# A second pick for the seven hottest tiles in a graph network kernel

## The reference, cut to what matters

```python
# first: attention of a kind, over the edges (row = src, col = dst)
h1   = relu(h[row] @ W1[:d] + h[col] @ W1[d:] + b1)
mask = sigmoid(h1 @ W2 + b2)[:, 0]
w    = mask / (segment_sum(mask, row)[row] + 1e-09)
agg  = segment_sum(w[:, None] * h[col], row)
out  = relu(where(deg > 0, 0.5 * h + 0.5 * agg, h) @ Wl + bl)
# second: four graph convolutions with a maximum over the neighbours
for W, R in (first, second, second, second):
    agg = segment_max(h[src], dst);  agg = where(isneginf(agg), 0, agg)
    h   = relu(agg @ W + b + h @ R)
```

## Time and profile before

| | before |
|---|---|
| median of three runs | 5941.76 us (5936.39 to 5943.95) |
| the profiled execution's own time | 5939.93 us |
| its span in the trace | 5938.1 us |
| busy: PE, DVE, POOL, ACT | 3743.0, 4317.3, 3295.4, 869.0 us |
| granted TensorE clock, mean | 0.869 |
| indirect gathers into `c_ring` | 1720 |
| gathers into `c_far_rows` | 16, 4 a layer |

### The profile page before, as it was taken

The page is one execution under the profiler, slowest core; times in us unless marked ns, Lnnn a source line. Parts: engine busy times, 40 slices in busy tenths (PEclk is TensorE's granted clock), DMA queues, the critical chain, the costliest instruction groups (busy, mean ns, idle before and its releaser), DMA issues. The chain is left out here.

```text
span 5938.1 us, 52093 instructions
## 1 busy us (share of the span) xinstructions
PE 3743.0 (63%) x16577; PEld 1793.4 (30%) x16577; DVE 4317.3 (73%) x7131; ACT 869.0 (15%) x2470; POOL 3295.4 (55%) x3349
## 2 busy tenths in 40 slices
PE   6670010565555542899997777757875777757775
PEld 5430010222222211444443333323332333323332
DVE  7789981876666652888886776758876887767775
ACT  0010001100000002777764100010000100010000
POOL 0210002477777774333332777767776777767776
PEclk9999995787878776999998888879998999978887
DMA  0129943644434434999997533334333433343332
GB/s 17 31 102 420 421 177 85 175 147 118 122 118 123 125 96 80 194 196 190 192 184 142 139 118 111 114 96 135 118 118 101 131 118 116 123 103 118 112 112 71
DMA packets 355334, 817.99 MB, mean 138 GB/s; under 512 B 95420, under 2 KB 209810, under 8 KB 354755
## 3 DMA queue, kind: packets, MB, share of 16 engines
q0 software_dynamic: 146496, 329.42, 25.5%
q1 hardware_dynamic: 159172, 406.54, 19.4%
q10 hardware_dynamic: 49392, 78.70, 4.6%
HBM read 579.98 MB, written 234.41 MB: 137 GB/s over the span
## 5 line engine op out<-in xcount | busy, mean ns | idle before, releaser
L2087 PE MATMUL c_wide<-c_choice,c_parts 128*128 128x512 fp8e4 (+1 forms) x8232 | 1766.9, 372 | 667.5 <-DVE c_even L2175 277.0
L1962 POOL DMA_INDIRECT c_ring<-table,near x1720 | 1649.3, 959 | 524.1 <-issue 523.5
L2087 PEld LDWEIGHTS c_wide<-c_choice,c_parts 128*128 128x128 bf16 x8232 | 810.6, 102 | 1598.9 <-issue 337.9
L2175 DVE TENSOR_TENSOR c_even<-c_even,c_wide 128x896 f32<-128x896 f32 x672 | 727.6, 1083 | 62.9 <-PE c_wide L2087 57.5
L2175 DVE TENSOR_TENSOR c_odd<-c_odd,c_wide 128x896 f32<-128x896 f32 x644 | 697.5, 1083 | 82.0 <-PE c_wide L2087 77.2
L2190 DVE TENSOR_REDUCE c_staged<-c_ring 128x128 f32<-128x1024 f32 (+15 forms) x196 | 400.4, 2043 | 413.2 <-DMA c_ring<-table,near 412.9
L1312 PE MATMUL a_wide<-a_choice,a_parts 128*128 128x512 fp8e4 (+1 forms) x2058 | 486.7, 385 | 337.6 <-DVE a_hidden L1398 312.6
L1702 PE MATMUL b_agg<-b_mass,b_h_row 128*128 128x512 f32 (+1 forms) x1372 | 592.9, 572 | 164.6 <-DMA b_mass<-masks 164.2
L1663 ACT ACTIVATE b_mass<-b_onehot,mask_r 128x128 f32<-128x128 bf16 x2058 | 625.5, 388 | 259.2 <-DVE b_onehot L1725 259.0
L1646 POOL DMA_DIRECT2D b_mass<-masks x343 | 296.4, 866 | 607.5 <-ACT b_mass L1663 580.2
L1191 POOL DMA_INDIRECT a_ring<-table_a,near x430 | 458.7, 1067 | 286.6 <-issue 130.4
(11 more groups left out here) (281 smaller groups left out, 3558.4 us busy)
## 6 DMA issues: line engine op xcount, KB each, us to landing
masks<-n_zeros SPq DMA_DIRECT2D x196, 784.0 KB, 15.2
b_mass<-masks POOLq DMA_DIRECT2D x343, 448.0 KB, 7.5
c_choice<-chosen SPq DMA_DIRECT2D x196, 784.0 KB
a_pick_row<-picks ACTq DMA_DIRECT2D x343, 224.0 KB, 3.7
chosen<-a_choice SPq DMA_DIRECT2D x49, 784.0 KB, 5.2
c_ring<-table,near POOLq DMA_INDIRECT x1720
c_source<-table SPq DMA_DIRECT2D x28, 448.0 KB, 6.5
a_ring<-table_a,near POOLq DMA_INDIRECT x430, 2.9
```

The source lines that it names most:

```text
L1962: pool.indirect_dma_start(ring[:, at + j, :], None, table1[layer % 2], bass.IndirectOffsetOnAxis(near[:, u, j:j + 1], 0)).then_inc(landed[ ...
L2087: last = pe.matmul(wide[q][:, lo_c:hi_c], parts[:, s, part, :], choice[e][:, s % CHUNK, lo_c:hi_c], start=(part == 0), stop=(part == 2))
L2175: dve.tensor_tensor(side[:, :], side[:, :], found, ALU.max).then_inc(taken, 1)
```

## The change

Four things change together.

- **A second pick.** The seven hottest tiles, one in each range, pick a second neighbour in each tile of sources. Their 7 x 128 columns form an eighth range, so `SELECTS` becomes 392. Their caps fall from 25, 16, 15, 14, 13, 13, 12 to 10, 8, 7, 7, 6, 6, 6, and `CAP_ALL` from 430 to 372. `list_again` removes the second picks from `near`, and `pick_again` finds them for `picks`. In stage B each range gets seven more blocks, which need no part of `masks`. In stage C the eighth range is done first in each layer (`range_at`), kept in `best_hot`, and put in by the second `take` of each other range.
- **Own rows by rank.** Stage B scatters `x` and `h1` by rank to `own_x` and `own_h` (`store_rows`, 98 indirect DMAs on POOL), in place of SP's store of `own1`. In layers 0 and 3 of stage C SP loads them with plain DMAs (`load_own`), in place of POOL's 98 gathers.
- **Lists that begin early.** `block_fetched` is split into seven semaphores, and DVE waits for the one that its pair of tiles needs.
- The ring of stage A shrinks from 38 entries to 36.

```diff
-CAP_BY_RANK = ((25, 16, 15, 14) + (13,) * 2 + (12,) * 3 + (11,) * 4 + (10,) * 5 + (9,) * 6 + (8,) * 6 + (7,) * 5
+CAP_BY_RANK = ((10, 8, 7, 7) + (6,) * 3 + (12,) * 2 + (11,) * 4 + (10,) * 5 + (9,) * 6 + (8,) * 6 + (7,) * 5
                + (6,) * 5 + (5,) * 4 + (4,) * 3 + (3, 2))
+ALL_RANGES = RANGES + 1
+ALL_TILES = TILES + RANGES
...
-                dve.wait_ge(block_fetched, TILES * 16)
                 for pair in range(0, TILES, 2):
                     both = range(pair, min(pair + 2, TILES))
+                    dve.wait_ge(block_fetched[both[-1] // PASS], PASS * 16)
...
+                hot = near[:, :, :].rearrange("p (a c) j -> p a c j", c=RANGE)[:, :, 0, :]
+                def list_again():
...
+                    for r in range(NEAR_ROUNDS):
+                        for a in range(RANGES):
+                            own.did(dve.max(top[:, a, 8 * r:8 * r + 8], work[r % 2][:, a, :]))
+                        if r < NEAR_ROUNDS - 1:
+                            for a in range(RANGES):
+                                own.did(dve.match_replace(work[1 - r % 2][:, a, :], top[:, a, 8 * r:8 * r + 8],
+                                                          work[r % 2][:, a, :], 0.0))
...
+                def pick_again():
+                    full = [P, PASS, RANGES * NEAR]
+                    for i in range(PASSES):
+                        tiles = slice(i * PASS, (i + 1) * PASS)
+                        own.did(dve.tensor_tensor(here[0][:, :, :], bc(hi_up[:, :].unsqueeze(1), full),
+                                                  bc(up_row[:, tiles].unsqueeze(2), full), ALU.is_equal))
+                        own.did(dve.tensor_tensor(here[1][:, :, :], here[0][:, :, :],
+                                                  bc(lo_up[:, :].unsqueeze(1), full), ALU.mult))
...
+                list_again()
...
+                own.did(dve.scalar_tensor_tensor(hot_far, hot_far, slow[:, :], hot_load[:, :], ALU.mult, ALU.add))
...
                 dve.sem_inc(laid_out, 1)
+                pick_again()
...
-        SELECTS = RANGES * TILES
+        SELECTS = ALL_RANGES * TILES
...
-        A_RING, A_FLOWS, A_LAG, A_BEHIND, A_PICKS = 38, 10, 5, 5, 6
+        A_RING, A_FLOWS, A_LAG, A_BEHIND, A_PICKS = 36, 10, 5, 5, 6
...
+            def wait_mass(eng, k):
+                if is_second(k):
+                    eng.wait_ge(weighed_made, k + 1)
+                    eng.wait_ge(rest_weighed, k + 1)
+                else:
+                    eng.wait_ge(mass_loaded[k % M_RING], (k // M_RING + 1) * 16)
...
+                def store_rows(cb, c):
+                    e = cb % 2
+                    pool.wait_ge(h1_made, cb + 1)
+                    by_rank_of = bass.IndirectOffsetOnAxis(rank[:, cb * RANGE + c:cb * RANGE + c + 1], 0)
+                    pool.indirect_dma_start(own_h, by_rank_of, h1[e][:, c, :], None).then_inc(rows_stored[e], 16)
+                    pool.indirect_dma_start(own_x, by_rank_of, x[e][:, c, :], None).then_inc(rows_stored[e], 16)
...
+                    if cb and ROWS_AT <= i < ROWS_AT + RANGE:
+                        store_rows(cb - 1, i - ROWS_AT)
+                for c in range(RANGE):
+                    store_rows(RANGES - 1, c)
...
-        STAGED_AT = tuple(REDUCED_AT[a * RANGE + RANGE - 1] for a in range(RANGES))
+        STAGED_AT = tuple(max(REDUCED_AT[a * RANGE + RANGE - 1], (a + 2) * TILES - 2) for a in range(RANGES))
...
+            def range_at(turn_no):
+                return turn_no - 1 if turn_no else RANGES
...
+                def load_own(layer, a):
+                    no, from_rows = (a, h_by_rank) if layer == 0 else (RANGES + a, x_by_rank)
...
+                    sp.dma_start(own_rows[no % 2][:, :, :], from_rows[a, :, :, :]).then_inc(own_loaded[no % 2], 16)
...
-                        if layer == LAYERS - 1:
...
-                            gather_own(RANGES + a, a, own1)
...
+                    if s == 1 and n > TILES:
+                        a = range_at(n // TILES)
+                        dve.tensor_tensor(side[:, 0:P], found[:, 0:P], best_hot[:, a * P:(a + 1) * P], ALU.max)
+                        dve.tensor_copy(side[:, P:RCOLS], found[:, P:RCOLS]).then_inc(taken, 1)
```

More of the change, by code:

```diff
@@ L770, in gnn @@
             laid_tile = sb("t_laid_tile", [1, QUICK_SLOTS // GROUP], I32)
-            picks_b = sb("p_picks_b", [P, TILES, P], BF16)
-            turned_b = sb("p_turned_b", [TILES, NODES_PAD], BF16)
+            picks_b = sb("p_picks_b", [P, ALL_TILES, P], BF16)
+            turned_b = sb("p_turned_b", [TILES, NODES_PAD + RCOLS], BF16)
+            hot_f = sb("s_hot_f", [P, RANGES, NEAR])
+            hi_i = sb("s_hi_i", [P, RANGES, NEAR], I32)
+            lo_i = sb("s_lo_i", [P, RANGES, NEAR], I32)
+            hi_up = sb("s_hi_up", [P, RANGES * NEAR], BF16)
+            lo_up = sb("s_lo_up", [P, RANGES * NEAR], BF16)
+            is_real = sb("s_is_real", [P, RANGES, NEAR])
+            again = sb("s_again", [P, RANGES, NEAR])
+            work = [sb(f"s_work{m}", [P, RANGES, NEAR]) for m in range(2)]
+            top = sb("s_top", [P, RANGES, NEAR])
+            empty = sb("s_empty", [P, RANGES, NEAR])
+            hot_load = sb("s_hot_load", [P, RANGES])
+            here = [sb(f"s_here{m}", [P, PASS, RANGES * NEAR >> max(m - 1, 0)], BF16) for m in range(4)]
+            second = sb("s_second", [P, TILES, RANGES])
             deg_t = ps("t_deg_t", [LTILES, P])
@@ L805, in _, with turn_picks @@
                 few = slice(0, LTILES)
-                pe.wait_ge(ready, 1)
-                for i in range(PASSES):
+                def turn_picks(i):
                     for q, first, n in HALVES:
@@ L834, in _ @@
                                  turned[q][0:TILES, 0:n, :].rearrange("p c m -> p (c m)")).then_inc(tile_copied[q], 1)
+                for i in range(PASSES):
+                    copy_picks(i)
                 act.wait_ge(info_made, 1)
@@ L1320, in dot_own @@
                 def dot_own(a):
-                    pe.wait_ge(bt_made, 2 * a + 2)
+                    pe.wait_ge(bt_made, min(2 * a + 2, 2 * RANGES))
                     if a:
                         pe.wait_ge(masks_made, a)
-                    for lo_c, hi_c in ((0, BANK), (BANK, RCOLS)):
-                        pe.matmul(logits[:, lo_c:hi_c], minus_w2[:, :],
-                                  minus_bt[:, a * RCOLS + lo_c:a * RCOLS + hi_c], start=True, stop=False)
+                    for h, first, count in HALVES:
+                        pe.matmul(logits[:, first * P:(first + count) * P], minus_w2[:, :],
+                                  minus_bt_of(a, first, count), start=True, stop=False)
                 def dot(a, first, count):
@@ L1589, in gnn @@
             stored = [sem(f"b_stored{e}") for e in range(2)]
+            rows_stored = [sem(f"b_rows_stored{e}") for e in range(2)]
             block = ctx.enter_context(nc.Block())
@@ L1899, in wait_table @@
                     eng.wait_ge(stored[1 - last % 2], stored_count(last - 1))
-            def over_layers(visit):
-                for layer in range(LAYERS):
-                    visit(layer)
+            def range_at(turn_no):
+                return turn_no - 1 if turn_no else RANGES
             @block.sync
```

275 lines of the change are left out of this document (181 added, 94 removed).

## The result

The changed kernel takes 6071.6 us (median; 6066.5 to 6076.3), the kernel before 5942.6 in the same comparison: ratio 1.0219 [1.0201, 1.0237], 129 us slower. I had forecast 6022 us, slower, in a range of 5920 to 6125.

A forecast was written before the change was run, and what follows sets the result against it. POOL was taken to bound stage A and the layers, but not stage B, where DMA and PE were busy. Terms 18 + 5 + 80 + 16 - 39 = +80 on 5941.8 gave 6022 us, range 5920 to 6125.

The forecast's parts named there:

- the count: Far loop: second-pick loads counted from the edges overflow five tiles by one entry each, so five passes replace one.
- Rival (a): Far loop in stages A and C: only one pass, the list count being wrong; 405 us fall away, 5617; chance 0.06.
- stage A's gathers: Stage A before its far loop: 58 fewer gathers and stores give -146, stops in the smaller ring +10.
- lists and picks: Listing and turning, before stage A: fetch wait goes, -34; second-pick work adds 52; sum +18.
- the far loop of A: End of stage A: four added passes at 35 us each, 141 us, for which all engines wait.
- the row scatters in stage B: POOL in stage B: 84 scatters covered by idle time among the blocks, the last 14 cost +16.
- the blocks: Stage B: 49 new blocks, PE setting the pace at 2.19 us a block, +80 (42 to 112).
- Rival (c): Stage B grows in full ratio (134, not 80) and POOL slows in stage A (+74): 6150; chance 0.15.
- the passes in C: Far loop in each layer: a pass costs its whole length, 16.5 us (15 to 19); four more, 66.
- rival (d): Added far-loop passes are short, both trips 3 us less; 16 passes give 96 us back: 5926; chance 0.08.
- Rival (b): Stage C: POOL, not the takes, bounds a layer, 560 + 66 = 626 us; total 5898; chance 0.09.
- The layers besides: Stage C: DVE's takes pace a layer, 549 of 657 us, 66 being added passes; four layers -39.

The follow-up runs named there:

- the last version: Changed kernel with full caps, row scatters spread, eight of fourteen a range paired behind blocks that load no mask, x's first at the end: 5698.2 us, 0.9590.

## Why the prediction was right, and where it was off

**Right: the count, and that it decides.** Five passes, from the largest loads against the caps. Four passes at 30.2 and 16 at about 12 are 121 + 193 = 314 us of the changed kernel, 304 by the run with five forced passes; without them it is 5751.6 us. Rival (a), one pass, was put at 5617, 135 us too low. The price of a pass has no part in that, since none is added there: stage B came 72 us above that forecast (1110.4 against 942.3 + 96), the layers without passes 35, stage A's gathers 20, five ring entries included.

**Right: lists and picks.** +21 for +18. The wait of 34.9 us went whole, and the experiment on it alone gives 31 to 35. The changed kernel's first gather comes 51.8 us behind that of the early lists alone (1054.2 against 1002.4): this is what `list_again` and `pick_again` add, forecast 52.

```profile
277.21 6.69 DVE L530 TENSOR_TENSOR record<-record,f_rstd 128x6272 f32<-128x6272 f32 x1
283.82 0.41 DVE L548 TENSOR_SCALAR n_valid<-iota_block,degree 128x64 f32<-128x64 f32 x2
```

**Right within 12 us: stage A's gathers**, -124 for -136. POOL resumes at 1143.24, 1174.88 and 1199.92, which with the lists' 21 us taken off is 1122, 1154 and 1179, where I had put 1120, 1152 and 1176. The first far gather came at 2182.5, 2161 with the 21 us taken off, for 2140 and 10 for stops. POOL's mean rose from 1.07 and 1.09 us to 1.10 and 1.11, 19 us over 744 DMAs, where the forecast's sum had left it as it was.

```profile
1143.24 1.14 POOL L1308 DMA_INDIRECT a_ring<-table_a,near  x1 [46.45 <-DVE a_value L1577]
...
1174.88 1.14 POOL L1308 DMA_INDIRECT a_ring<-table_a,near  x1 [18.86 <-DVE a_value L1577]
...
1199.92 1.14 POOL L1308 DMA_INDIRECT a_ring<-table_a,near  x1 [13.97 <-DVE a_value L1577]
```

**A term mis-sized: the far loop of A**, 30.2 us a pass for 35. I had taken the slots' trip of 6.1 us from the earlier trace rows; in the second pass it is 2.5 (load issued at 2210.46, gather at 2213.00). From that gather to the last addition are 25.0 us for 24.75, and from there to the next load of slots 3.5 for 4.3.

**The step that failed: the row scatters in stage B.** The prediction reads: "Of them 84 lie among the blocks, where POOL is idle two thirds of the time; uncovered they would delay 42 mask loads by 1.3 us each, 55 us." The idle share is a mean over the range. The scatters don't use it: they stand behind seven blocks in a row, two for each, and there a turn of the queue is a mask load and two scatters, 1.29 + 1.30 + 0.96 = 3.6 us at the least (no pause of 0.3 stands between a scatter and the mask load behind it), for a block of 2.2. DVE, four blocks ahead, and the ring of eight masks cover only a part. Of the 75 us, 21 lie at the end and 54 among the blocks: the uncovered price, 55, was right. At the end the last h1 is stored at 3426.66 and the block behind begins at 3452.06, 25.4 us later, where the kernel before took 4.5 us from its stores at 3256.05 to 3260.51: 21 for the forecast 16. First the changed kernel, then the kernel before:

```profile
3426.66 0.37 SPq L1763 DMA_DIRECT2D table<-b_h  x1
3426.91 1.04 POOL L1783 DMA_INDIRECT own_h<-b_h,rank  x1 [42.76 <-ACT b_h L1808]
...
3443.45 0.95 POOL L1784 DMA_INDIRECT own_x<-b_x,rank  x1 [0.30 <-issue]
3452.06 0.35 SPq L2064 DMA_DIRECT2D c_w<-in_L_gnn_W  x1
```

```profile
3256.05 0.37 SPq L1624 DMA_DIRECT2D own<-b_x  x1
...
3260.51 0.35 SPq L1908 DMA_DIRECT2D c_w<-in_L_gnn_W  x1
```

**A term mis-sized: the blocks**, +80, measured 92 to 99. A range without row scatters takes 1041.1 / 7 = 148.7 us; if its end still takes 23, a block takes 2.24 us for my 2.19, an estimate. Rival (c), full ratio, had 134 and was too high.

**A term mis-sized: the passes in C.** 16.5 us each, measured 11.8 to 12.5. The row was a first pass. There the slots' load, 6.1 us to POOL's gather, is issued right behind two loads of sources of 448 KB, as it is in the first passes of the changed kernel (5.0 to 5.2 in layers 1 to 3); in a repeated pass it takes 2.5 to 2.7. The gathers, 6.0 from the last issue to DVE, take 4.85. That isn't a matter of the first pass, which has 4.7 to 5.3 in these layers too. The kernel before had 5.9 to 6.4 in all four layers, with other gathers right behind; a layer's fifth pass has gathers behind it as well and takes 4.9 to 5.8, so they can be a part of it. The rest stays open. This was the mechanism of rival (d), 3 us less on each trip: 3.5 and 1.2 came.

The Trainium skill (DMA: Bandwidth & Descriptors, Anatomy of one DMA) gives about 2.0 us fixed for a DMA issued by GpSimd. The gathers' 4.85 us is over twice that. The prediction held the slots' trip against it too, but SyncE issues that load, which the section isn't about. Rival (d) put the kernel at 5926, too low by 146, of which 78 lie in stage B, 25 in the passes of C and most of the rest in the layers' other work.

**The layers besides.** Without the added passes, a layer is (2610.8 - 193) / 4 = 604 us, forecast 657 - 66 = 591; where the 13 us lie wasn't followed. Rival (b), layers paced by POOL, had 560 without them; it fails, and the chain has PE and DVE in POOL's place. What I had said would show it, "POOL idle in the layers, for ring entries", is wrong. The groups of the four layers:

```profile
L2130 POOL DMA_INDIRECT c_ring<-table,near x1488 | 1447.4, 973 | 453.4 <-issue 450.7 <-DVE c_staged L2355 2.7
L2355 DVE TENSOR_REDUCE c_staged<-c_ring 128x128 f32<-128x768 f32 (+10 forms) x196 | 351.0, 1792 | 37.9 <-DMA c_ring<-table,near 37.9
L2141 POOL DMA_INDIRECT table<-c_new,row_info x147 | 141.6, 963 | 190.2 <-ACT c_new L2199 148.5 <-issue 41.8
```

POOL waits 2.7 us for ring entries and DVE 37.9 for gathers; POOL's free time is at the layer's end, 148.5 us before the stores. DVE is busy 537 of 650 us, 82%, not over 85. The two are nearly in step: the 49 gathers of own rows cost 43 of their 62 us when put back. Own rows by rank thus bring 86 us in the layers and cost 75 in stage B as they were made, 38 when spread and some 27 in the last version.

**The chance given.** Faster had 0.17 and slower 0.77. The balance hung on 300 us of passes, which the count of the lists decides. The rest of the sum was not that safe: the error in stage B, 78 us, is as large as the whole change that was forecast, 80, and the sign held because this error pointed upward. That the time came within 50 us is in part luck: 78 us in stage B, 48 in the layers' other work and 15 in the lists and stage A's gathers were too little, and the passes, 91 us too dear in all, made up for most of it.

## What to carry to other kernels

- A fixed capacity is worth a count on the data: one entry too few in five of 49 lists costs 304 us, where five entries more cost some 10 us in stage A and nothing that shows in the layers. The overflow path is dear because the kernel puts it where all engines wait for it.
- Idle share on a queue covers added work only where the idle time is. Compare the turn of the queue where the work is put with the time of a step there; a burst of two beside each load cost 54 us, the same work one at a time 12 to 19 (31 and 38 in all, less 19 at the end).
- A first pass of a loop, behind other loads, prices no repeated pass: look for the row in which nothing stands ahead.

## What the runs showed that I had not expected

In setting A the same kernel before took 7383 us (7352 to 7413) instead of 5942, and the order of the versions turned over: the fastest, 0.959 elsewhere, is 1.011 [1.0085, 1.0142] there. The record's chip numbers don't tell the two settings apart: 3 and 5 stand at sets with 7383 and 7387 us and also at sets with 5941 and 5944. So whether it is the chip or something else at the time isn't shown. Stage B takes the same, 1113.6 and 1110.4 us with caps that fit, but the gathers of stage A take 1392 us for 1136, and the layers 3922 for 2408. A window of 500 us inside the layers of this kernel, first in setting A, then in the other:

```profile
4200.00:4700.00 500.00, 277.25 (x1226) 128.76 (x1226) 258.00 (x241) 22.24 (x34) 208.69 (x219) 0.77 0.27 77
```

```profile
3440.00:3940.00 500.00, 439.58 (x2227) 220.97 (x2225) 452.35 (x419) 23.02 (x42) 349.49 (x364) 0.97 0.45 132
```

One operation is as long as elsewhere (a take 1.09 us), but 241 DVE records take the time of 419: between the takes lie gaps of 5 to 16 us on DVE, up to 32 on PE, and the trace names no transfer that ends them. It puts 15% of the chain that ended last down to "another core or an unknown queue", which the chain of the other setting doesn't have. The row ends a gap in which DVE and PE both stand:

```profile
4317.37 1.09 DVE L2337 TENSOR_TENSOR c_even<-c_even,c_wide 128x896 f32<-128x896 f32 x1 [15.02 <-issue]
```

The stages that are much longer are those of the selects and takes, of which the change has 8 for 7. That fits the turned order, but no run tells what the gaps are: this stays open.
